# Shared expert's down products of six token groups: full float32 products or three products of rounded parts

## The reference, cut to what matters

```python
gs = jnp.einsum('bsd,fd->bsf', hidden_states, Ws_g)
us = jnp.einsum('bsd,fd->bsf', hidden_states, Ws_u)
shared = jnp.einsum('bsf,df->bsd', gelu(gs) * us, Ws_d)
return out + shared          # out: the 16 experts' part
```

## Time and profile before

| | us |
|---|---|
| median of 3 runs (lowest, highest) | 1725.29 (1721.97, 1725.39) |
| the profiled execution's own time | 1727.6 |
| its span in the profile | 1725.9 |
| TensorE busy, share of the span | 1630.6, 94% |
| VectorE busy, share of the span | 1212.9, 70% |
| ScalarE busy, share of the span | 736.3, 43% |
| this stage (first to last matmul of it) | 1265.3 to 1427.0 |

### The profile page before, as it was taken

The page is one execution under the profiler, slowest core; times in us unless marked ns, Lnnn a source line. Parts: engine busy times, 40 slices in busy tenths (PEclk is TensorE's granted clock), DMA queues, the critical chain, the costliest instruction groups (busy, mean ns, idle before and its releaser), DMA issues. The chain is left out here.

```text
span 1725.9 us, 25574 instructions
## 1 busy us (share of the span) xinstructions
PE 1630.6 (94%) x9280; PEld 1383.8 (80%) x9280; DVE 1212.9 (70%) x2669; ACT 736.3 (43%) x1447; POOL 543.0 (31%) x443
## 2 busy tenths in 40 slices
PE   7999989989999999999979999999989999999996
PEld 4688878878878888867867888888768788989895
DVE  6877677765445656646797999999867935666663
ACT  3333333434333334435426666666521324454442
POOL 2100020000000002332434666666400024777764
PEclk9999999999999999999999999999999999999998
DMA  6000000000010010031115222232141125666653
GB/s 226 4 1 1 1 1 1 1 25 25 0 50 1 1 13 13 19 107 55 33 50 204 66 77 77 79 90 79 58 160 50 49 64 151 147 152 158 140 120 37
DMA packets 80248, 111.55 MB, mean 65 GB/s; under 512 B 15982, under 2 KB 60154, under 8 KB 79868
## 3 DMA queue, kind: packets, MB, share of 16 engines
q1 hardware_dynamic: 66172, 91.43, 16.6%
q0 software_dynamic: 12288, 17.31, 5.6%
q10 hardware_dynamic: 1664, 1.18, 0.2%
HBM read 81.59 MB, written 27.68 MB: 63 GB/s over the span
## 5 line engine op out<-in xcount | busy, mean ns | idle before, releaser
L3037 POOL DMA_INDIRECT out<-k_eo,idx x64 | 117.2, 1832 | 75.4 <-DVE k_eo L3129 60.7
L1926 POOL DMA_INDIRECT k_xe<-rows_dram,idx x64 | 82.5, 1288 | 179.0 <-DVE idx L2970 140.7
L1759 PE MATMUL d_pO<-d_sp,d_raw 128*128 128x257 f32 x512 | 114.6, 380 | 3.4 <-DVE x L1211 3.3
L1759 PEld LDWEIGHTS d_pO<-d_sp,d_raw 128*128 128x128 f32 x512 | 95.7, 189 | 17.8 <-DVE x L1211 4.1
L537 ACT ACTIVATE b_p<-b_pS,b_nmax 128x2048 f32<-128x2048 f32 (+14 forms) x32 | 40.6, 1270 | 142.0 <-DVE b_nmax L678 142.0
L61 PE MATMUL b_pO<-b_vh,b_ph 128*128 128x256 f32 x302 | 87.9, 291 | 4.7 <-DVE b_pl L660 4.6
L62 PE MATMUL b_pO<-b_vh,b_pl 128*128 128x256 f32 x302 | 85.5, 283 | 0.0
L63 PE MATMUL b_pO<-b_vl,b_ph 128*128 128x256 f32 x302 | 85.4, 283 | 0.0
L333 POOL TENSOR_TENSOR x<-x,b_vrow 128x256 f32<-128x256 f32 x32 | 24.0, 782 | 190.8 <-DVE b_hs L606 190.7
L2119 ACT ACTIVATE g_dlm<-d_cumb,mod 128x128 f32<-128x128 f32 x256 | 78.5, 395 | 2.9 <-DMA d_cumb<-cum_dram 2.9
L3088 ACT ACTIVATE k_act_g<-k_pg 128x512 f32<-128x512 f32 x64 | 38.3, 599 | 88.6 <-PE k_pu L63 88.6
(11 more groups left out here) (565 smaller groups left out, 5345.7 us busy)
## 6 DMA issues: line engine op xcount, KB each, us to landing
d_cumb<-cum_dram SPq DMA_DIRECT2D x32, 512.0 KB, 4.3
k_wf<-in_WgT SPq DMA_DIRECT2D x16, 512.0 KB, 3.9
k_wf<-in_WuT SPq DMA_DIRECT2D x16, 512.0 KB, 4.9
k_wf<-in_WdT SPq DMA_DIRECT2D x16, 512.0 KB, 7.0
rows_dram<-h_hx SPq DMA_DIRECT2D x32, 136.0 KB, 3.9
x<-in_x SPq DMA_DIRECT2D x8, 512.0 KB, 9.6
d_w<-in_w SPq DMA_DIRECT2D x4, 1024.0 KB, 6.2
uT_dram<-d_ug SPq DMA_DIRECT2D x16, 256.0 KB, 2.4
```

The lines of the kernel that those rows point to most:

```text
L1759: last = nc.tensor.matmul(pO[:, t % 2, 0:PW], raw[e][:, t * P:(t + 1) * P], proc[e], start=e == 0, stop=e == E - 1)
L1926: nc.gpsimd.indirect_dma_start(out=m.xe[:, e % 2, t, :], out_offset=None, in_=m.rows, in_offset=bass.IndirectOffsetOnAxis(ap=column(m, e, ...
L3037: nc.gpsimd.indirect_dma_start(out=out, out_offset=bass.IndirectOffsetOnAxis(ap=column(m, e, t), axis=0), in_=eo[:, e % 2, t, :], in_offse ...
```

## The change

The down products of groups 2 to 7 (EXACT = 2) are made of rounded parts with `exact_matmul`; groups 0 and 1 stay as they were. For that

- VectorE's multiplication writes its product over the gelu in `act_g`, and not into `hid`; ScalarE rounds it into `hidh` (`hidden_high`, behind the gelu of the same slice in its queue), and VectorE writes the low part `hidl` (`hidden_low`, at the gate piece of the next slice, behind `side(k)`). That is 24 slices;
- the down weights are split once for each batch: `down_high` on ScalarE at n = 4 and n = 8, `down_low` on VectorE behind the residual additions of groups 0 and 1, over the float32 weights;
- TensorE waits ahead of the first down tile for the low parts of three slices, and ahead of the second for that of the fourth. `QUADS` orders the 16 products so that the fourth slice is first needed in the second of four parts;
- ScalarE's gelu of slice n waits for the low part of slice n - 2, since the buffer of `act_g` is read until then.

```diff
+        wdl = [again("wdl0", [P, FT, C], m.wd_at), again("wdl1", [P, FT, C], nc.sbuf_base - FT * C * 4)]
+        wdh = [again(f"wdh{b}", [P, FT, C], m.x_at + (16 + 4 * b) * 1024) for b in range(B)]
+        hidh, hidl = again("hidh", [P, B, FT, GW], hid_at), again("hidl", [P, FT, GW], m.x_at + 8 * 1024)
...
+        EXACT = 2
+        split = lambda n: max(n - EXACT * FT, 0)
+        QUADS = [[(0, 0), (0, 1), (0, 2), (2, 0)], [(2, 1), (2, 2), (0, 3), (1, 0)], [(1, 1), (1, 2), (1, 3), (2, 3)], [(3, f) for f in range(FT)]]
...
+            def hidden_high(n):
+                g = n // FT
+                act.wait_ge(s["hid_done"], made(n + 1))
+                act.wait_ge(s["o_ready"], g - 1)
+                nc.scalar.copy(hidh[:, g % B, n % FT], act_g[:, n % 2]).then_inc(s["hh_done"], 1)
+            def down_high(b):
+                act.wait_ge(s["hid_done"], made((b + 1) * FT))
+                if b:
+                    act.wait_ge(s["gain"], 1)
+                nc.scalar.copy(wdh[b][:], wd[b][:]).then_inc(s["wdh_done"], 1)
...
                 act.wait_ge(s["hid_done"], made(n - 1))
+                act.wait_ge(s["hl_done"], split(n - 1))
                 nc.scalar.activation(act_g[:, n % 2], pg[:, n % 2], ACT.Gelu).then_inc(s["gelu_done"], 1)
+                if n // FT >= EXACT:
+                    hidden_high(n)
+                if n == FT:
+                    down_high(0)
+                if n == 2 * FT:
+                    down_high(1)
                 if n % FT == 0 and n // FT + 1 < NJ:
                     next_high(n // FT + 1)
...
-                    pe.wait_ge(s["hid_done"], made((g + 1) * FT))
+                    if g < EXACT:
+                        pe.wait_ge(s["hid_done"], made((g + 1) * FT))
+                    else:
+                        pe.wait_ge(s["hl_done"], split((g + 1) * FT) - 1)
+                        pe.wait_ge(s["wdl_done"], min(g - EXACT + 1, B))
...
+                if t == 1 and g >= EXACT:
+                    pe.wait_ge(s["hl_done"], split((g + 1) * FT))
...
+                        tt, f = QUADS[t][i]
+                        tok = slice(tt * P, (tt + 1) * P)
+                        last = exact_matmul(nc, po[:, tt], hidh[:, g % B, f, tok], hidl[:, f, tok], wdh[g % B][:, f, :], wdl[g % B][:, f, :],
+                                            f == 0, f == FT - 1)
...
+            def hidden_low(n):
+                g, f = n // FT, n % FT
+                dve.wait_ge(s["hh_done"], split(n + 1))
+                if g > EXACT:
+                    dve.wait_ge(s["o_ready"], g)
+                v.tensor_tensor(hidl[:, f], act_g[:, f % 2], hidh[:, g % B, f].bitcast(F32), ALU.subtract).then_inc(s["hl_done"], 1)
+            def down_low(b):
+                dve.wait_ge(s["wdh_done"], b + 1)
+                v.tensor_tensor(wdl[b][:], wd[b][:], wdh[b][:].bitcast(F32), ALU.subtract).then_inc(s["wdl_done"], 1)
...
                 side(k)
+                if not half and n > EXACT * FT:
+                    hidden_low(n - 1)
                 if half:
                     dve.wait_ge(s["gelu_done"], made(n + 1))
-                    dve.wait_ge(s["o_ready"], max(g - 1, 0))
-                    v.tensor_tensor(hid[:, g % B, f], act_g[:, f % 2], pu[:, f % 2], ALU.mult).then_inc(s["hid_done"], 1)
+                    if g < EXACT:
+                        dve.wait_ge(s["o_ready"], max(g - 1, 0))
+                    v.tensor_tensor(act_g[:, f % 2] if g >= EXACT else hid[:, g % B, f], act_g[:, f % 2], pu[:, f % 2],
+                                    ALU.mult).then_inc(s["hid_done"], 1)
...
             def down(g, t, k):
                 side(k)
+                if t == 0 and g == NJ - 1:
+                    hidden_low(NJ * FT - 1)
...
+                    if g < EXACT:
+                        down_low(g)
```

## The result

| | before | changed |
|---|---|---|
| median (lowest, highest), us | 1725.4 (1721.97, 1728.51), 9 runs | 1729.86 (1727.57, 1733.12), 9 runs |
| span of the profiled execution, us | 1725.9 | 1730.9 |

The ratio is 1.0027, with a 95% interval of 1.0015 to 1.0038: the changed kernel takes 2.6 to 6.6 us more.

What follows compares the result with a forecast made beforehand. TensorE was taken to bound the stage, with VectorE's queue level through the tables. Table products 5.5 us late, less what groups 6 and 7 recover, gave +3.8 on 1725.3, so 1729.1; range 1722.5 to 1734.

Steps and rivals of the forecast that it cites:

- its own spread of 2.5 us: Uncertainty given to the whole forecast, either way, as a sum of a dozen waits each known to 0.2 or 0.3.
- The products, 1.08 us a group: TensorE's down products in groups 2 to 7: 5.75 us a group with rounded parts instead of 6.83, saving 1.08.
- The three quarters: Rival: rounded down products cost three quarters of plain ones, 5.12 us a group, giving 1714; chance 0.02.
- The counting stretch: Up to k = 44: VectorE's additions make sums 0.6, then 1.7 late, group 3's end 0.3, last decision 1.5.
- The table stretch: k = 44 to 70: VectorE's full queue makes the last table 7.5 us late, TensorE's table products 5.5.
- The clock: TensorE's clock may halve behind waits of 2.4 and 2.5; the loss goes into the next wait, upper bound 3.4.
- The fourth wait, 1.4 ahead of slice 24: One of four TensorE stands forecast on the way to the table products: 1.4 us ahead of slice 24.
- The end of the stage: Behind the tables: TensorE leaves group 6 5.1 late and group 7 3.8 late, and the experts follow unchanged.
- The last step of the sum: Group 7 saves 1.08 and swaps its earlier 0.65 wait for about 0.6, leaving TensorE 3.8 late.
- The rival that TensorE keeps its 7.2 us: VectorE's additions fit beside TensorE if they add less than 2.8 us by the last table: 1718; chance 0.12.
- the waits for roundings: VectorE's subtractions of slices 19, 21 and 23 each wait 0.76 for ScalarE's rounding, 2.3 in the table stretch.
- the rival of a cheaper detour: Counting stretch hides its additions, subtractions find roundings done; 1.5 and 2.3 fall away: about 1725; chance 0.2.

Runs made afterwards that it cites:

- e3_plain_products: Changed kernel with all roundings, subtractions and waits kept, but plain float32 down products of the high parts; 1733.12 us, ratio 1.0035 to the kernel before.
- e9: Changed kernel with the down weights' two subtractions moved on VectorE to the third down tile of the next group; 1728.66 us, ratio 1.0006 to the kernel before.
- e4: Changed kernel without the 24 subtractions of the products, the high part standing in for the low; 1724.04 us, ratio 0.9976 to the kernel before.
- e8: Kernel before the change, with 3 of 16 down products left out in each of groups 4 and 5; 1724.89 us, ratio 0.9991 to the kernel before.
- e2: Changed kernel with each product's subtraction moved half a piece back, to the next slice's up piece; 1730.69 us, ratio 1.0015 to the kernel before.
- e1: Changed kernel with all 24 product subtractions and the weights' two moved from VectorE to GpSimd; 1734.81 us, ratio 1.0043 to the kernel before.
- e5: Kernel before, with rounded products in groups 6 and 7 only and the weights' low parts on GpSimd; 1722.35 us, ratio 0.9980 to the kernel before.
- e7: Changed kernel with the down weights' two subtractions on GpSimd instead of VectorE; 1732.04 us, ratio 1.0035 to the kernel before.
- e6: Same as e5, with slice 25's subtraction put behind the product of slice 26; 1722.87 us, ratio 0.9981 to the kernel before.

## Why the prediction was right

The forecast was +3.8 us, and 3.47 reach the experts in the trace. The ratio gives 4.7, with an interval of 2.6 to 6.6. The mechanism is the forecast one: VectorE's full queue makes the last table late, and with it the table products. That the sum came within 0.4 us is partly luck, by its own spread of 2.5 us and by the slips below. Point by point:

- **The products, 1.08 us a group.** Right: 0.12 a matmul, and `e3_plain_products` loses 3.41 without them. The three quarters that the prediction estimates from the Trainium skill's four passes ("FP8 and Floating Point Precision", TensorE Precision Notes) are not there in this trace: 0.122 x 48 = 5.8 us, and not 5.12.
- **The counting stretch.** The sum behind `down_low` of batch 0 was 0.5 late (forecast 0.6), that behind batch 1's 1.7 (1.7: 34.32 from the first down against 32.60). `e9` takes the second away (1.69). The end of group 3's down products: 0.58 late (0.3). The last decision: 1.63 late (1.5), and `next_low` did wait for `next_high` ahead of it, 0.51 at 1344.05.
- **The table stretch.** The last table 7.61 late (7.5), the table products 5.53 (5.5). The waits: 2.25 ahead of the second part of group 4's (2.4), 2.22 ahead of slice 23 (2.5), 0.96 ahead of group 5's second part (1.4). The list of TensorE's waits left one out: 1.34 for the sum at 1352.53, 0.41 before. And their total in the stage is 11.1, where "about 15" was forecast. VectorE was not without idle time: it waited 0.69 for a rounding three times, as the sum has it.
- **The clock.** The fourth wait, 1.4 ahead of slice 24, isn't there. In its place the granted clock fell to 0.50, the 1.2 GHz level, behind the wait at 1376.66: eight matmuls lay 0.43 apart instead of 0.23, 1.6 us. TensorE came to slice 24 at 1381.11, about when the product it needs (1380.10, and 0.74 more) was there. This is what the forecast said of it, that the loss goes into the next wait. Without the fall TensorE would have been there at 1379.5 and waited to 1380.84, so by this estimate the fall cost some 0.3.
- **The end of the stage.** Group 6 is left 4.93 late (5.1), group 7 3.50 (3.8). The last step of the sum has a slip: 5.1 - 1.08 - 0.65 + 0.6 is 4.0 and not 3.8, and the wait of before is 0.53 in its trace and not 0.65. Slice 28 waits 0.70 and group 7's second part 0.48 (0.6).

**Where the working was too coarse.** The terms add up well, but they are not prices that can be taken back one at a time. The rival that TensorE keeps its 7.2 us was put at the condition that VectorE's last table is less than 2.8 us late. In `e4` it is 1.88 late, and TensorE gets 2.83 in place of 7.2, nearly all of it behind the tables. `e8`, with no addition at all, loses half of a saving ahead of the tables. So the condition as I wrote it was wrong: with VectorE's queue level with TensorE's already before, all that group 4 saves was not to be had even with nothing added; for groups 2 and 3 no run shows how much was. The second thing that I left out is what stands behind a rounding on ScalarE: I named `next_high` and the last scaling, but not the gelus, which `e4` shows to make the next product 0.87 late. Third, the waits for roundings were right in size (2.3 forecast in the table stretch, 2.1 measured), but the rival of a cheaper detour counted them as time that falls away from the chain; `e2` removes most of them and gains 0.37.

**What stays open.** The medians differ by 4.5, the traces by 3.47 and the 0.45 + 1.1 that lie ahead of the first down product. The 1.1 is not the change's: five of the kernels with its additions do not have it. The interval of 2.6 to 6.6 holds 3.47 alone, so nothing in the medians asks for more. The clock's fall in the table stretch was read in one execution of each kernel; how often it comes is not known. And the price of ScalarE's part alone is not shown, since `e1`, which was to show it, put a new stop in its place.

## What to carry to other kernels

An engine at 94% doesn't own every stretch: before counting a saving, look at each stretch for a second engine that runs level, and relieve the first at the second's cost only in stretches where the second has room; here that is two groups of six, and it turns +0.3% into -0.2% (`e5`). When an operation is made cheaper by a detour over two other engines, count three things: what it adds to their queues, the latency of the detour (1.36 us from product to subtraction against 0.60 in a full queue), and what stands behind the waiting instruction. An idle engine is not always a free place for work: here GpSimd, reading its operands from SBUF, stopped VectorE. Try one instruction first.

## What the runs showed of the hardware

**GpSimd and VectorE stop each other.** In `e7` a VectorE instruction of 128x1 elements with two operands in SBUF took 2.22 us instead of 0.16, ending with GpSimd's instruction; in `e1` a table of 2.29 took 3.39, and GpSimd's subtraction 2.63 instead of 1.27. The Trainium skill ("SBUF — State Buffer", Who interferes with whom) says that an instruction of VectorE with two inputs in SBUF and one of GpSimd that reads SBUF exclude each other for the whole instruction. The trace agrees, down to a VectorE instruction of a single element for each partition. The weights' low parts of `e5` are in GpSimd's queue too (2.38 and 2.80 us, from 1382.98 on), behind the last table, and `e5` gains all that was expected of it.

**The clock behind a wait.** A wait of 2.25 us at 1364.38 was followed by a granted clock of 1.00, one of 2.22 at 1376.66 by 0.50 from about 1377.7 on. `e1`, `e2`, `e3`, `e7` and `e9`, with longest waits of 1.9 to 3.0 us in the table stretch, show at least one such fall each there; `e4`, `e5`, `e6` and `e8`, whose longest are 1.6 to 1.7, show none. The 2.25 us without a fall, here and once in `e9` (2.26 at 1360.59), show that the length of the wait alone doesn't settle it.
